# Attention scores made a second time with keys on the partitions, in place of transposed probabilities

## The reference

```python
latent = einsum('bld,dc->blc', x, Wkv_down)
k = einsum('blc,chk->blhk', latent, Wk_up); v = einsum('blc,chk->blhk', latent, Wv_up)
attn = einsum('bqhd,bkhd->bhqk', einsum('bld,dhk->blhk', x, Wq), k) / sqrt(64)
attn = softmax(where(causal, attn, neg_inf), axis=-1)
y = einsum('bhqk,bkhd->bqhd', attn, v)
out = einsum('bqhd,hdo->bqo', y, Wout)
```

## Time and profile before

| | |
|---|---|
| median of 3 runs | 3190.7 us (3187.5 to 3202.6) |
| profiled execution | 3181.0 us, span 3179.0 us, mean granted TensorE clock 0.888 |
| TensorE matmul / weight load busy | 2622.8 (83%) / 2124.4 us (67%) |
| VectorE / ScalarE / GpSimd busy | 2036.4 (64%) / 1808.9 (57%) / 853.9 us (27%) |
| costliest lines | L446, L435, L426, L457: 540, 457, 381, 428 us busy |

### The profile page before, as it was taken

The page is one execution under the profiler, slowest core; times in us unless marked ns, Lnnn a source line. Parts: engine busy times, 40 slices in busy tenths (PEclk is TensorE's granted clock), DMA queues, the critical chain, the costliest instruction groups (busy, mean ns, idle before and its releaser), DMA issues.

```text
span 3179.0 us, 76627 instructions
## 1 busy us (share of the span) xinstructions
PE 2622.8 (83%) x26192; PEld 2124.4 (67%) x26193; DVE 2036.4 (64%) x5025; ACT 1808.9 (57%) x4422; POOL 853.9 (27%) x1042
## 2 busy tenths in 40 slices
PE   3999898988989997986886289999999978958882
PEld 2777777777777776775765166667666657857671
DVE  2777666776766765874554666666766647855555
ACT  2777777777777775552444265555665545534441
POOL 0000000000000002663555232342442315744551
PEclk9999999999999997666999599899999876669996
DMA  6323323332332221111222200000000001112225
GB/s 147 48 42 45 48 41 51 49 46 42 49 44 41 41 41 36 40 43 54 69 68 71 88 2 2 2 2 2 2 2 2 2 2 35 41 46 68 70 69 171
DMA packets 117817, 140.22 MB, mean 44 GB/s; under 512 B 21324, under 2 KB 79825, under 8 KB 117360
## 3 DMA queue, kind: packets, MB, share of 16 engines
q1 hardware_dynamic: 100592, 101.63, 17.2%
q0 software_dynamic: 16896, 34.12, 3.2%
HBM read 45.85 MB, written 40.54 MB: 27 GB/s over the span
## 4 chain that ended last, share of the span: by engine, by line
PE 50%; DVE 18%; issue 12%; ACT 9%; another core or an unknown queue 5%; DMA 2%; SPq 1%; DVEq 1%; POOL 1%; ACTq 0%; POOLq 0%
PE psum L457 5%; PE psum L426 5%; PE psum L492 4%; ACT probs L446 3%; PE psum L1515 3%; DVE state L1718 3%; DVE neg_max L435 2%; PE psum L1563 2%; DVE x_sb L1288 2%; PE psum L543 2%; PE psum L1137 2%; PE psum L1432 2%; PE psum L1125 2%; PE psum L304 2%
## 5 line engine op out<-in xcount | busy, mean ns | idle before, releaser
L446 ACT ACTIVATE probs<-psum,neg_max 128x512 f32<-128x512 f32 (+3 forms) x1024 | 539.8, 538 | 244.3 <-DVE neg_max L435 243.5
L435 DVE TENSOR_REDUCE neg_max<-psum 128x1 f32<-128x512 f32 (+3 forms) x1024 | 457.3, 483 | 54.0 <-PE psum L427 24.9
L426 PE MATMUL psum<-ls,qs 96*128 96x512 f32 (+3 forms) x1024 | 380.9, 397 | 112.4 <-ACT probs L446 96.5
L457 PE MATMUL psum<-ident,probs 128*128 128x128 f32 x2560 | 428.4, 283 | 2.9 <-ACT probs L446 0.8
L1250 POOL DMA_INDIRECT y_tok<-yb,xb x272 | 267.7, 984 | 301.5 <-DVE yb L1225 226.6
L426 PEld LDWEIGHTS psum<-ls,qs 96*128 96x128 f32 x1024 | 198.2, 194 | 216.8 <-ACT probs L446 158.4
L325 POOL TENSOR_TENSOR rstd<-var_eps,half_neg 128x4 f32<-128x4 f32 x32 | 40.1, 1254 | 1103.1 <-DVE var_eps L321 1103.1
L476 DVE COPY probs_t<-psum 128x512 f32<-128x512 f32 (+1 forms) x384 | 230.4, 600 | 147.5 <-PE psum L457 140.4
L457 PEld LDWEIGHTS psum<-ident,probs 128*128 128x128 f32 x2560 | 273.7, 144 | 26.1 <-ACT probs_t L472 10.1
L914 POOL DMA_INDIRECT x_slot<-pay,pos_i x256 | 256.3, 1001 | 129.8 <-issue 76.1
L427 PE MATMUL psum<-causal_r,ident_r 128*128 128x128 f32 x1024 | 235.4, 242 | 0.0
(11 more groups left out here) (320 smaller groups left out, 6748.8 us busy)
## 6 DMA issues: line engine op xcount, KB each, us to landing
qs<-q_h SPq DMA_DIRECT2D x128, 256.0 KB, 5.5
xb<-x_slot SPq DMA_DIRECT2D x272, 66.0 KB
qs<-q_l SPq DMA_DIRECT2D x64, 256.0 KB, 5.7
y<-y_tok SPq DMA_DIRECT2D x32, 512.0 KB, 3.5
y_tok<-yb,xb POOLq DMA_INDIRECT x272
x_sb<-in_x SPq DMA_DIRECT2D x16, 256.0 KB, 5.5
x_slot<-pay,pos_i POOLq DMA_INDIRECT x256
out<-x_sb SPq DMA_DIRECT2D x16, 256.0 KB, 2.9
```

The lines of the kernel that those rows point to most:

```text
L426: pe.matmul(o[:, at:at + n], q, ls[par][0:3 * LD, 0:n], start=(at == 0), stop=False, skip_group_check=True)
L435: last = dve.tensor_reduce(neg_max[:, par, h, qt:qt + 1], bank[u % 3][:, at:at + (qt + 1) * P], AX.X, ALU.max, negate=True)
L446: last = act.activation(probs[:, u % 3, c], bank[u % 3][:, c], ACT.Exp, bias=neg_max[:, par, h, qt:qt + 1], accum_out=row_sum[:, par, h, q ...
L457: last = pe.transpose(bank[3 + u % 2][:, c:c + P], probs[:, u % 3, c:c + P], ident[:, :])
```

## The change

It removes the transposes of probabilities (L457), their copies (L472, L476), the row sums beside the exponential, and the two turns of y. The first scores are made as before, 20 units ahead (AHEAD), into 2 banks, with one mask product for each unit (DIAG), whose maxima of 128-key blocks one VectorE instruction takes for a whole bank. Four small reductions join them for a group of heads; they are transposed, copied, and brought by one DMA as row 96 into `qs`, against a row of ones in `ls`. Then scores are made again, with keys on the partitions and the maxima subtracted by that row (`keys_tensor`), into 3 banks; ScalarE writes the exponential straight into `probs_t`; GpSimd sets the entries above the diagonal to zero (`mask_gpsimd`); values follow as 16 products for a group, and 16 more with ones give the sums (`sums_tensor`). The sums are turned, inverted, spread by GpSimd, turned back, and multiplied with y on VectorE. Token latents are made from `ls` by a product with a 0/1 matrix (`pick_r`), 4 matmuls for 12. LayerNorm's statistics and norm are spread over several steps. Tables for this are made at the start of the stage. Elsewhere only semaphores are renamed or merged. ScalarE's order at a step is: exponential, split of a projection (one step after it), copy of the maxima (step 6), of y (3), of the sums (7), LayerNorm's (11 of group 0).

```diff
+KEY_TILES = [[(0, 0)], [(3, 0), (1, 128)], [(2, 0)]]
+DIAG = [(384, P), (256, 2 * P), (P, P)]
+TILE_MAX = [(3, 0), (2, 4), (0, 7), (1, 8)]
+KEY_AT = {kb: (k, at) for k, tiles in enumerate(KEY_TILES) for kb, at in tiles}
...
+        def proj_tensor(pe, b, par, item):
             if item == 0:
                 pe.wait_ge(s["ln_lo"], b + 1)
+            else:
                 pe.wait_ge(s["q_lo"], b * A_ITEMS + item)
             if item == 0:
+                last = mm3(pe, ln_bank[0:KEYS, :], wkv_h[:, 0:3, :].rearrange("p r c -> p (r c)"),
                            wkv_l[:, 0:3, :].rearrange("p r c -> p (r c)"), xh[par][:, :], xl[par][:, :])
             elif item == 1:
                 for t in range(QT):
+                    last = pe.matmul(ln_bank[:, t * LD:(t + 1) * LD], ls[par][0:KEYS, t * P:(t + 1) * P],
+                                     pick_r[0:KEYS, :], start=True, stop=True)
...
         def scores_tensor(pe, b, par, u):
             h, k = divmod(u, UNITS)
             g = h // HG
+            o = bank[u % 2]
+            if u % GU == 0:
                 pe.wait_ge(s["q_dma"], (b * G + g + 1) * 16 * Q_DMAS)
+            positive(pe, "s_max", b * UPS + u - 1)
             for qt, at in UNIT_TILES[k]:
                 n = (qt + 1) * P
+                pe.matmul(o[:, at:at + n], qs[0:KEYS, h, qt * P:(qt + 1) * P], ls[par][0:KEYS, 0:n],
+                          start=(at == 0), stop=False, skip_group_check=True)
+            at, n = DIAG[k]
+            pe.matmul(o[:, at:at + n], ident_r[:, :], causal_r[:, 0:n], start=False, stop=True,
+                      skip_group_check=True).then_inc(s["s_mm"], 1)
+        def max_vector(dve, b, u):
             h, k = divmod(u, UNITS)
+            g, j = divmod(h, HG)
+            n = UNIT_COLS[k] // P
             dve.wait_ge(s["s_mm"], b * UPS + u + 1)
+            dve.tensor_reduce(block_max[:, g % 2, j, k * QT:k * QT + n],
+                              bank[u % 2][:, 0:UNIT_COLS[k]].rearrange("p (n c) -> p n c", c=P), AX.X,
+                              ALU.max).then_inc(s["s_max"], 1)
+        def max_join_vector(dve, b, g):
+            dve.wait_ge(s["s_max"], b * UPS + (g + 1) * GU)
+            positive(dve, "mx_mm", b * G + g - 1)
+            for qt, at in TILE_MAX:
+                last = dve.tensor_reduce(neg_max[:, g % 2, 0:HG * QT].rearrange("p (j t) -> p j t", t=QT)[:, :, qt],
+                                         block_max[:, g % 2, :, at:at + qt + 1], AX.X, ALU.max, negate=True)
+            last.then_inc(s["mx_red"], 1)
+        def max_turn_tensor(pe, b, g):
+            pe.wait_ge(s["mx_red"], b * G + g + 1)
+            positive(pe, "mx_out", b * G + g)
+            pe.transpose(ln_bank[:, 0:P], neg_max[:, g % 2, :], ident[:, :]).then_inc(s["mx_mm"], 1)
+        def max_copy_scalar(act, b, g):
+            act.wait_ge(s["mx_mm"], b * G + g + 1)
+            positive(act, "mx_dma", (b * G + g) * 16)
+            act.activation(max_t[0:HG * QT, :], ln_bank[0:HG * QT, 0:P], ACT.Copy).then_inc(s["mx_out"], 1)
+        def max_sync(sp, b, g):
+            done = b * G + g + 1
+            if not isinstance(b, int):
+                done = sp.to_reg(done)
+            sp.wait_ge(s["mx_out"], done)
+            sp.dma_start(qs[KEYS:KEYS + 1, g * HG:(g + 1) * HG, :].bitcast(F32),
+                         max_t[0:HG * QT, :].bitcast(F32)).then_inc(s["mx_dma"], 16)
+        def keys_tensor(pe, b, par, u):
             h, k = divmod(u, UNITS)
+            o = bank[2 + u % 3]
+            if u % GU == 0:
+                pe.wait_ge(s["mx_dma"], (b * G + h // HG + 1) * 16)
+            positive(pe, "s_exp", b * UPS + u - 2)
+            for kb, at in KEY_TILES[k]:
+                n = L - kb * P
+                last = pe.matmul(o[:, at:at + n], ls[par][0:KEYS + 1, kb * P:(kb + 1) * P], qs[0:KEYS + 1, h, kb * P:L],
+                                 start=(at == 0), stop=True, skip_group_check=True)
+            last.then_inc(s["k_mm"], 1)
+        def exp_scalar(act, b, u):
             h, k = divmod(u, UNITS)
...
+            g, j = divmod(h, HG)
+            if u % GU == 0:
+                positive(act, "sum_mm", b * G + g - 1)
+            act.wait_ge(s["k_mm"], b * UPS + u + 1)
+            act.activation(probs_t[:, g % 2, j, UNIT_AT[k]:UNIT_AT[k] + UNIT_COLS[k]], bank[2 + u % 3][:, 0:UNIT_COLS[k]],
+                           ACT.Exp).then_inc(s["s_exp"], 1)
+        def mask_gpsimd(pool, b, u):
+            h, k = divmod(u, UNITS)
+            g, j = divmod(h, HG)
+            n = len(KEY_TILES[k])
+            pool.wait_ge(s["s_exp"], b * UPS + u + 1)
+            pool.sem_inc(s["go_pool"], 1)
+            blocks_k = probs_t[:, g % 2, j, UNIT_AT[k]:UNIT_AT[k] + n * P]
+            pool.affine_select(out=blocks_k, in_=blocks_k, compare_op=ALU.is_ge, fill=0.0, base=0, pattern=[[0, n], [1, P]],
+                               channel_multiplier=-1).then_inc(s["p_done"], 1)
+        def values_tensor(pe, b, par, g, kb):
+            if kb == 0:
+                pe.wait_ge(s["p_done"], b * UPS + (g + 1) * GU)
+                positive(pe, "y_ev", b * G + g)
+                if g == 1:
+                    positive(pe, "x_done", b)
+            k, at = KEY_AT[kb]
+            c = slice(UNIT_AT[k] + at, UNIT_AT[k] + at + L - kb * P)
+            for j in range(HG):
+                last = pe.matmul(bank[5][j * LD:(j + 1) * LD, kb * P:L], lat_tok[par][:, kb, :], probs_t[:, g % 2, j, c],
+                                 start=(kb == 0), stop=(kb == QT - 1), skip_group_check=True)
+            if kb == QT - 1:
                 last.then_inc(s["pv_mm"], 1)
...
+        def sums_tensor(pe, b, g, kb):
+            if kb == 0:
+                positive(pe, "y_norm", b * G + g)
+            k, at = KEY_AT[kb]
+            c = slice(UNIT_AT[k] + at, UNIT_AT[k] + at + L - kb * P)
+            for j in range(HG):
+                last = pe.matmul(bank[6][j * LD:(j + 1) * LD, kb * P:L], ones_f[:, :], probs_t[:, g % 2, j, c],
+                                 start=(kb == 0), stop=(kb == QT - 1), skip_group_check=True)
+            if kb == QT - 1:
+                last.then_inc(s["sum_mm"], 1)
...
+        def sum_copy_scalar(act, b, g):
+            act.wait_ge(s["sum_mm"], b * G + g + 1)
+            positive(act, "inv_mm", b * G + g)
+            act.activation(sum_t[:, :], bank[6][:, :], ACT.Copy).then_inc(s["sum_ev"], 1)
+        def sum_back_tensor(pe, b, g):
+            pe.wait_ge(s["sum_ev"], b * G + g + 1)
             for t in range(QT):
...
+        def sum_inv_vector(dve, b, g):
+            dve.wait_ge(s["sum_back"], b * G + g + 1)
+            positive(dve, "inv_wide", b * G + g)
+            dve.reciprocal(r_inv[:, :, :], bank[6][:, :].rearrange("p (t j c) -> p t j c", t=QT, j=HG)[:, :, :, 0]
+                           ).then_inc(s["y_rinv"], 1)
+        def inv_wide_gpsimd(pool, b, g):
+            pool.wait_ge(s["y_rinv"], b * G + g + 1)
+            pool.sem_inc(s["go_pool"], 1)
+            pool.tensor_copy(sum_t[:, :].rearrange("p (t c) -> p t c", c=LD), r_inv[:, :, :].rearrange("p t (j o) -> p (t j) o", o=1)
+                             .to_broadcast([P, QT * HG, LD])).then_inc(s["inv_wide"], 1)
+        def inv_fwd_tensor(pe, b, g):
+            pe.wait_ge(s["inv_wide"], b * G + g + 1)
             for t in range(QT):
...
+        def y_norm_vector(dve, b, g):
+            dve.wait_ge(s["inv_mm"], b * G + g + 1)
+            dve.wait_ge(s["y_ev"], b * G + g + 1)
+            if g == 0:
+                positive(dve, "o_mm", b)
+            dve.tensor_tensor(y_n[:, g, :], bank[6][:, :], y_t[:, :], ALU.mult).then_inc(s["y_norm"], 1)
+        def out_tensor(pe, b, t, following=1):
+            if t == 0:
+                pe.wait_ge(s["y_norm"], b * G + G)
+                pe.wait_ge(s["y_ev"], b * G + G + following)
+            for g in range(G):
+                last = pe.matmul(bank[5][:, t * P:(t + 1) * P], y_n[:, g, t * P:(t + 1) * P], wvo[:, g, :],
+                                 start=(g == 0), stop=(g == G - 1))
+            if t == QT - 1:
+                last.then_inc(s["o_mm"], 1)
...
+        AHEAD = 20
+        LN_STATS, LN_NORM, LN_TURN = 1, 8, 10
+        PROJ_AT = {(0, 1): A_ITEMS - 1, (1, 0): 0, (1, 2): 1, (1, 7): 2, (2, 7): 3, (3, 7): 4}
+        MAX_AT = 5
+        PV_AT, SUMS_AT = 2, 6
+        INV_AT = 1
...
+            def values_at(b, par, g, v):
+                if v == PV_AT:
+                    for kb in range(QT):
+                        values_tensor(pe, b, par, g, kb)
+                if v == SUMS_AT:
+                    for kb in range(QT):
+                        sums_tensor(pe, b, g, kb)
+                if v == SUMS_AT + 2:
+                    sum_back_tensor(pe, b, g)
             def batch(b, par, nxt, proj):
                 for u in range(UPS):
+                    g, v = divmod(u, GU)
+                    if u + AHEAD < UPS:
+                        scores_tensor(pe, b, par, u + AHEAD)
```

(96 more changed lines are left out.)

365 lines of the change are left out of this document (107 added, 258 removed).

## The result

The changed kernel takes 3266.8 us, median of four runs (3260.0 to 3290.2), against 3196.7 of four runs of the kernel before (3187.5 to 3203.0): a ratio of 1.024, 95% interval 1.018 to 1.029. It is slower by some 70 us, clear of the noise. The profiled execution took 3260.0 us around a span of 3258.3; before it was 3181.0 and 3179.0.

A forecast was written before the change was run, and what follows sets the result against it. No engine was full: a ring of scores, maximum and exponential left 11.7 us of waits in a 70.1 us sequence. 3181 + 26 (sixteen sequences) + 5 (ends) = 3212, at the median's level 3222, stated as 3220; range 3070 to 3300.

The forecast's parts named there:

- the forecast's own case: Whole kernel: the likeliest case, 3180 to 3265 us, set beside three rivals and given chance 0.43.
- TensorE's work: Attention stage, per sequence at full clock: stays the same within half a microsecond, 58.4 us before and 58.8 after.
- Those two terms: TensorE's value products and sums by a matrix of ones: 2.5 us a group each, the sums adding 10 a sequence.
- ScalarE, VectorE, GpSimd: Busy time a sequence: ScalarE from 53 to some 30 us, VectorE from 51 to some 40, GpSimd 14 to 19.
- The walk of waits: New waits through a group of twelve steps: 15.2 us a group, 70.9 a sequence with output, norm, queries and loop turn.
- norm and latents: Next sequence's norm and latents' split: waits of 1.3 and 1.2 us, with 1.1 of late maxima 3.6 a sequence.
- late maxima: VectorE's maxima queued behind q_l: late by 1.1 us at steps 11 to 1 of a group.
- The sum at full clock: One sequence: 70.9 us and 0.8 for issue gaps, 71.7 against 70.1; times 16, plus 26 us.
- The second rival: Slower: the transfer of queries decides, with 2 us of transfer and one half-clock stretch a sequence; 3300 us, chance 0.20.
- The ends: Start and drain of the attention stage: first keys wait 12 us, partly covered, mask tables add 2 to 3; plus 5.
- The first rival: The waits dissolve: a sequence takes 62 to 65 us, the kernel 3090, or 3050 to 3165 with part; chance 0.33.
- two banks and nine steps for a transfer: Argument against the waits dissolving: only two banks hold first scores, and a query transfer of 7.8 us has nine steps.

The follow-up runs named there:

- E1: Changed kernel with the projections of query groups 2 and 3 moved from step 7 to step 3: 3273.7 us, 1.027 of the kernel before; attention stage alone 1281.5 us.
- E7: Changed kernel, only reordered: norm, projections of groups 2 and 3, join and splits earlier, selecting product and turn of sums later; 3117.1 us, 0.974 of the kernel before.

## Why the prediction was right in direction and short in size

3220 us was forecast, 3070 to 3300; it came out at 3267, slower as forecast, and 47 above. The forecast loss was 29 us (3220 for 3191) and the measured one 70, so the size was less than half of it, and the time lies just above the forecast's own case of 3180 to 3265. Step by step:

**TensorE's work, right.** The value block: 642.28 to the next start at 644.57 is 2.29 a group; 2.5 was taken, between 2.2 and 3.1.

```profile
641.73 0.62 PE L388 MATMUL psum<-pick_r,ls 96*128 96x32 f32 x4 [1.51 <-DVE ls L411]
642.28 2.36 PE L521 MATMUL psum<-probs_t,lat_tok 128*32 128x512 f32 x32
644.57 0.38 PE L439 MATMUL psum<-ls,qs 96*128 96x256 f32 x1
...
647.41 0.30 PE L465 MATMUL psum<-ident,neg_max 128*128 128x128 f32 x1 [0.94 <-issue]
```

The sums take the same. Those two terms were 0.4 a group too high, 1.7 a sequence; busy time at 2.4 GHz fell by 2.1 where plus 0.4 was forecast.

**ScalarE, VectorE, GpSimd, right.** 32.6, 38.8 and 18.9 us busy a sequence, for 30, 40 and 14 to 19. A selection takes 0.29 us for 128 columns and 0.41 for 256, 0.33 in the mean. A maximum of a full bank stands 0.61 before what follows it (0.60 forecast). Four joins take 0.37 by their records and 0.28 to the next start (0.32 forecast):

```profile
680.78 0.69 DVE L450 TENSOR_REDUCE block_max<-psum 128x4 f32<-128x512 f32 x1 [2.06 <-PE psum L442]
681.39 0.37 DVE L458 TENSOR_REDUCE neg_max<-block_max 128x4 f32<-128x16 f32 x4
681.67 0.68 DVE L450 TENSOR_REDUCE block_max<-psum 128x4 f32<-128x512 f32 x1
```

**The walk of waits, right in kind, with one of them oversized.** Per sequence: queries 2.0 (1.4 in the sum), the turn of the maxima 1.6 (2.2), norm and latents 2.7 (3.6 less the late maxima of 1.1), late maxima 1.0 (1.1 in each group and once more behind the latents, 5.5), the turn of the sums 0.65 (not forecast). ScalarE's q_h waits 3.4 us for the landing, but once in two sequences, at the loop's turn, where TensorE's idle time is 4.90 for 2.83: 1.0 a sequence where 2.5 was forecast. With the queries landed earlier (E1) that turn is back at 2.87. The recorded sum has two slips: the wait for the queries is said to come "in two groups of four" and enters once, 1.4 for 2.8, and the group's "14.1 is work" holds a wait, for its parts add up to 13.3.

**The sum at full clock, right, in part by luck.** Take the stretches at 1.2 GHz off at half their length, the most that they can cost, and twelve sequences take 847.5 us before and 860.9 after: 70.6 and 71.7 each, at the least. 71.7 was forecast. But idle time grew by 3.2 a sequence where the sum had 1.2, and work shrank by 2.1 where it had plus 0.4.

**The term that failed: the clock.** The sum was made at full clock and let the kernel before's difference between the two kinds of sequence stand ("71.7 against 70.1, plus 1.6, times 16"). It held no half-clock stretch beyond those of before. Measured, 8.8 us of a sequence stand at 1.2 GHz in place of 3.4: up to 2.7 a sequence, 43 in sixteen. The second rival had this mechanism, "one half-clock stretch a sequence", at 3 us. What came is the forecast's waits with the second rival's clock. The choice to treat them as either one or the other was the error: 78.5 of the 105.8 us at 1.2 GHz stand at the waits for the queries and the loop's turns (last section), both of which the sum had counted as waits alone.

**The ends, too small.** Plus 5 was forecast, and 6 for the four sequences outside the twelve; 36.5 was measured: the third output comes 52.2 us later, and from the fifteenth to the last it takes 15.7 less. Here too half the added time at 1.2 GHz, 30.7 us in the record of the clock, accounts for up to 15. That record begins late, at 104.9 us (before: 75.3), and until then 512-column starts lie 0.43 apart: the clock first rises 29.6 us later than in the kernel before, which is up to 15 more. The first scores start at 60.67 and the first keys come at 84.94, 24 us later, where 12 were forecast, since the twenty units run at 1.2 GHz. The wait of 6.99 among them is no part of the loss, for the kernel before has one of 7.27 at the same place:

```profile
60.67 0.63 PE L439 MATMUL psum<-ls,qs 96*128 96x512 f32 x1
...
69.24 0.58 PE L439 MATMUL psum<-ls,qs 96*128 96x256 f32 x1 [6.99 <-DVE block_max L450]
...
84.94 0.73 PE L488 MATMUL psum<-qs,ls 97*128 97x512 f32 x1
...
101.91 0.63 PE L308 MATMUL psum<-x_pad,wkv_l 128*96 128x512 f32 x1
102.34 0.63 PE L309 MATMUL psum<-x_pad,wkv_h 128*96 128x512 f32 x1
```

**The first rival** said 62 to 65 us a sequence if the waits dissolve. As the change was ordered they did not; in E7 they did, at 63.3 between the turns, and the whole kernel took 3117 where the rival's 3090 was worked out. What it spoke for, twenty units of lead, was there. What stood against it, two banks and nine steps for a transfer, was a matter of where the steps lie, not of the arithmetic.

## What to carry to other kernels

Taking a third of the work off engines that are not full brings nothing by itself; look for the points of the new order at which one wait ends last, and walk each of them. Idle time on TensorE is priced twice, once as the wait and once as the slower clock that may follow it: here 1.1 us a sequence of net waits and work became 3.8. And before a reordered kernel is given up, move its steps: the same operations took 3267 us in one order and 3117 in another.
